# Windowed attention and mixed FFN on one core: projection weights in four column pieces, mixed-weight halves taken two steps behind, third pair's maxima sent ahead of the first loads of v

## The chip, the cores and the metric

The kernel runs on one NeuronCore of a Trainium2 chip, as one program. The core has a matrix engine (TensorE, PE in the profile; its weight loads are PEld), a vector engine (VectorE, DVE), a scalar engine (ScalarE, ACT), GpSimd (POOL) and SyncE (SP), which here only issues transfers. The metric is the device time of one execution in microseconds. Three runs of the kernel before took 3001.5, 3004.55 and 3013.76 us; the median is 3004.55 us.

## The reference, cut to what matters

```python
x = x + layernorm(attn(layernorm(x), w_qkv))       # x: 4 x 2048 x 512, w_qkv: 512 x 1536
x = x + layernorm(ffn(layernorm(x), ...))

# attn: 16 heads of 32 columns; queries in windows of 128 rows, each against the window
#       before, its own and the one after (384 keys; none beyond the ends of a sequence)
qkv = x @ w_qkv;  scores = (q * 32**-0.5) @ k_ctx.T;  out = softmax(scores) @ v_ctx

# ffn, per batch b of 4, with 8 experts
g   = mean over tokens of (relu(x @ gate_w1.T + gate_b1) @ gate_w2.T + gate_b2)   # 4 x 8
mW1 = W1 + sum_e g[b, e] * TW1[e];   mW2 = W2 + sum_e g[b, e] * TW2[e]            # F = 2048
u   = gelu(x @ mW1.T + b1 + g @ Tb1);   out = u @ mW2.T + b2 + g @ Tb2
```

Everything is float32. A layernorm is over the 512 columns.

## The kernel before, in words

Nearly every product is made three times to keep float32 accuracy: each operand is split into a high part (rounded to the matrix engine's `fp32r` by a copy on ACT) and a low part (the rest, a subtraction on DVE), and PE adds high by high, high by low and low by high. Every engine runs a fixed, written order of instructions; semaphores alone hold them together.

**Projection (to 581 us).** Sixteen chunks of 512 tokens. For each chunk DVE takes the row statistics and normalises (`take_stats`, `normalise_x`), PE transposes four blocks (`turn_block`, L529), ACT and DVE split them into `xt_hi` and `xt_lo` (`xt_block`, L346 and L441), and PE makes twelve groups of twelve products (`group`, L534): groups 0 to 3 are q, 4 to 7 are k (group g takes columns 128g to 128g+127 of the weights), groups 8 to 11 are v (columns 1024 to 1535). Groups 4 to 7 are followed by the transposes of the next chunk. Group 4 reuses the PSUM bank of group 0, and so waits until ACT and DVE have taken group 0 out.
Before the first chunk the weights are loaded by SP in four row blocks `k` of 128 rows and all 1536 columns (L233), right behind the first rows of x. ACT copies each block to `w_hi` (L378), DVE subtracts it for `w_lo` (L491). Both stand ahead of the first `xt_block` on their engines, and PE waits for all four before its first group (L665). The square root of the first statistics (L342) is the first activation of the program.

**Attention (581 to 1301 us).** Steps T, one pair of windows each. In step T PE makes the scores of pair T+3 (`score`, L585), the key products of pair T (`keys`, L602) and the output of pair T-2 (`values`, `sums`, L631, L639). DVE takes the maxima of the scores (`reduce`, L467); PE turns them (L610), DVE copies them to `max_rows` (L474) and SP sends them by two small transfers into one extra row of `q_st` (`row`, L228). `keys(g, 4)`, in the middle of a pair's eight, waits for the row of pair g+1. SP issues everything in its own order: at the change from projection to attention it sends the last stores of v (L201), then four loads of v of 256 KB (L215), then goes on with step 0, whose `row` is that of pair 2.

**Gate and FFN (1301 us to the end).** First sixteen chunks of normalising and gate. Then 256 steps s of about 5.4 us. A step is one block of 128 of the 2048 hidden columns, for one chunk of 512 tokens; two blocks are a run, so each odd step ends one. PE makes `hidden(s + 2)` (L1242 to L1244), then `project(s)` (L1259 to L1261). ACT makes gelu and high part of step s+2 (`hidden_block`, L1357, L1361); at the end of a run `next_run` copies four sums out (L1374) and puts the next four into PSUM (L1385), for which PE waits before the next `project`; three steps behind the last run of a chunk it normalises four tiles (`normalise`, L1399), after POOL has made the shift (L1132 to L1139) from DVE's statistics (L1586, L1589). DVE makes the low part `u_lo` of step s+2 (`low_hidden`, L1577) and, up to three times in a step, adds one expert to both halves of a weight block (`mix`, L1553, two instructions).
`mix_plan` gives, by fixed costs, the step `done[n]` in which weight block n has had its eight experts. `ready_by` says in which step the finished block is split: ACT makes `w_hi` (`high_weights`, L1350) and DVE `w_lo` (`low_weights`, L1572). A block that is wanted within two steps is split at the head of the step; else ACT does it behind `hidden_block` and `next_run` and ahead of `normalise`, and DVE behind the first addition of the step. A block is first used by `hidden` two steps ahead of its own step.

## Time and profile before

| | |
|---|---|
| runs | 3001.5, 3004.55, 3013.76 us; median 3004.55 |
| profiled execution | 3006.66 us; span of the instructions 3004.9 us |
| PE busy | 2890.8 us, 96% |
| DVE, ACT, POOL busy | 1988.1 (66%), 1727.3 (57%), 842.0 us (28%) |
| mean granted TensorE clock | 0.984 of 2.4 GHz |

PE is busy almost throughout, so the time is PE's work, the spans in which it waits, and the spans in which its granted clock is 0.50 (1.2 GHz) instead of 1.00 (2.4 GHz). What the other engines do costs only where PE waits for it. A busy PE's matmul ends are modelled, so the distance from start to start says more than the duration. "Idle before" in a row is the time the engine stood still ahead of it, with the engine and line that released it.

### The profile page before, as it was taken

To read this page: it belongs to the slowest core of one execution; us is meant where nothing else is said; L and a number is where in the kernel's file an instruction comes from. 1 tells how busy PE (TensorE), PEld (TensorE's weight loads), DVE (VectorE), ACT (ScalarE), POOL (GpSimd) and SP (SyncE) were. 2 spreads that over 40 slices of the span, in tenths; PEclk is the share of its full clock that TensorE was granted. 3 is DMA by queue.
4 is the path that set the end of the run, shared out by engine and by line. 5 is a ranking of instruction groups with operands and counts; after the bars stand their busy time and mean duration, and the time that the engine had idled before them with its cause. 6 is when DMAs were issued, how large, how long until landed. Compare 5 with 4: busy or idle time off the path is not lost.

```text
span 3004.9 us, 55697 instructions
## 1 busy us (share of the span) xinstructions
PE 2890.8 (96%) x20444; PEld 2414.2 (80%) x20444; DVE 1988.1 (66%) x3750; ACT 1727.3 (57%) x3384; POOL 842.0 (28%) x694
## 2 busy tenths in 40 slices
PE   7999999999999999959989999999999999999998
PEld 6888888788888888848777888888887888878886
DVE  4333333488877888858857767776669766786664
ACT  2222222376666667645645666766667666676665
POOL 1000000088888888853310000310005000040003
PEclk9999999999999999979999999999999999999999
DMA  5554555677887888769999766886669756896632
GB/s 194 184 180 169 176 187 199 203 181 188 195 187 188 195 196 193 172 206 389 381 359 345 258 231 228 330 318 234 218 216 392 255 201 215 287 358 214 238 133 84
DMA packets 363587, 697.06 MB, mean 232 GB/s; under 512 B 26424, under 2 KB 125752, under 8 KB 363336
## 3 DMA queue, kind: packets, MB, share of 16 engines
q1 hardware_dynamic: 342848, 646.15, 66.8%
q10 hardware_dynamic: 16416, 31.98, 3.0%
q0 software_dynamic: 4080, 15.73, 1.3%
q8 instruction: 148, 2.42, 0.3%
q14 instruction: 95, 0.78, 0.1%
HBM read 525.45 MB, written 167.78 MB: 231 GB/s over the span
## 4 chain that ended last, share of the span: by engine, by line
PE 45%; DMA 4%; ACT 2%; DVE 2%; issue 1%; POOL 1%; SPq 1%; POOLq 0%; ACTq 0%; DVEq 0%
PE e_hid L1242 7%; PE e_hid L1243 7%; PE e_hid L1244 7%; PE e_acc L1259 7%; PE e_acc L1260 7%; PE e_acc L1261 7%; DMA yl_scratch<-e_yt_lo 3%; POOL e_c_x L1127 1%; DVE e_part L1553 0%; SPq L1011 0%; ACT e_yt_hi L1321 0%; DVE e_c_stats L1476 0%; ACT e_sums L1374 0%; DMA e_att<-o_scratch 0%; ACT e_sums L1399 0%
## 5 line engine op out<-in xcount | busy, mean ns | idle before, releaser
L1553 DVE SCALAR_TENSOR_TENSOR e_part<-e_ring,e_g_cols,e_part 128x512 f32<-128x512 f32 x896 | 642.2, 776 | 3.8 <-DMA e_ring<-mix_rows 1.6
L467 DVE TENSOR_REDUCE a_neg_max<-a_ps_score 128x1 f32<-128x384 f32 (+1 forms) x1024 | 492.7, 527 | 67.4 <-PE a_ps_score L585 55.7
L312 POOL TENSOR_TENSOR a_total<-a_probs 128x512 f32<-128x512 f32 x256 | 323.7, 1281 | 620.2 <-ACT a_probs L397 620.2
L397 ACT ACTIVATE a_probs<-a_ps_keys 128x384 f32<-128x384 f32 (+1 forms) x1024 | 426.8, 478 | 56.5 <-PE a_ps_keys L602 29.5
L1357 ACT ACTIVATE e_u<-e_hid,e_mb 128x512 f32<-128x512 f32 x256 | 177.4, 693 | 446.3 <-PE e_hid L1244 440.2
L1577 DVE TENSOR_TENSOR e_u_lo<-e_u,e_u_hi 128x512 fp32r<-128x512 f32 x256 | 182.4, 712 | 317.3 <-ACT e_u_hi L1361 317.0
L1132 POOL TENSOR_SCALAR e_var<-e_moments 128x4 f32<-128x4 f32 x15 | 8.5, 566 | 1297.6 <-DVE e_moments L1589 1297.0
L602 PE MATMUL a_ps_keys<-a_q_st,a_k_st 97*128 97x384 f32 (+1 forms) x1024 | 314.2, 349 | 20.6 <-DMA a_q_st<-a_max_rows 18.9
L585 PE MATMUL a_ps_score<-a_k_st,a_q_st 96*128 96x384 f32 (+1 forms) x1024 | 326.6, 357 | 0.6 <-DVE a_neg_max L467 0.5
L322 POOL TENSOR_TENSOR a_total<-a_total,a_probs 128x512 f32<-128x512 f32 x224 | 286.2, 1278 | 68.8 <-ACT a_probs L397 66.3
L447 DVE TENSOR_TENSOR a_qk<-a_acc,a_qk 128x512 fp32r<-128x512 f32 x128 | 88.4, 690 | 315.8 <-ACT a_qk L353 315.8
L1374 ACT ACTIVATE e_sums<-e_acc 128x512 f32<-128x512 f32 x508 | 289.1, 595 | 5.7 <-PE e_acc L1261 5.7
L1385 ACT ACTIVATE e_acc<-e_sums 128x512 f32<-128x512 f32 x448 | 263.7, 614 | 0.0
L353 ACT ACTIVATE a_qk<-a_acc 128x512 fp32r<-128x512 f32 x128 | 76.6, 598 | 266.3 <-PE a_acc L534 266.3
L602 PEld LDWEIGHTS a_ps_keys<-a_q_st,a_k_st 97*128 97x128 f32 x1024 | 190.6, 191 | 34.5 <-DMA a_q_st<-a_max_rows 27.2
L585 PEld LDWEIGHTS a_ps_score<-a_k_st,a_q_st 96*128 96x128 f32 x1024 | 191.9, 190 | 27.7 <-DVE a_neg_max L467 16.9
L1259 PE MATMUL e_acc<-e_wa_hi,e_u_hi 128*128 128x512 f32 x512 | 201.5, 394 | 6.8 <-ACT e_acc L1385 6.8
L534 PE MATMUL a_acc<-a_xt_hi,a_w_hi 128*128 128x512 f32 x512 | 204.7, 400 | 1.4 <-DVE a_xt_lo L441 1.4
L1242 PE MATMUL e_hid<-e_y_hi,e_wb_hi 128*128 128x512 f32 x512 | 200.0, 391 | 2.3 <-DVE e_wb_lo L1572 2.3
L1242 PE MATMUL e_hid<-e_y_hi,e_wa_hi 128*128 128x512 f32 x512 | 200.7, 392 | 0.8 <-DVE e_x L1532 0.8
L1260 PE MATMUL e_acc<-e_wa_lo,e_u_hi 128*128 128x512 f32 x512 | 200.9, 392 | 0.0
L1261 PE MATMUL e_acc<-e_wa_hi,e_u_lo 128*128 128x512 f32 x512 | 200.6, 392 | 0.0
(147 smaller groups left out, 6510.4 us busy)
## 6 DMA issues: line engine op xcount, KB each, us to landing
e_ring<-mix_rows SPq DMA_DIRECT2D x558, 512.0 KB, 5.3
qk_scratch<-a_qk SPq DMA_DIRECT2D x128, 512.0 KB, 3.0
a_k_st<-qk_scratch SPq DMA_DIRECT2D x180, 256.0 KB, 4.3
a_q_st<-qk_scratch SPq DMA_DIRECT2D x180, 256.0 KB, 4.3
a_x_in<-x SPq DMA_DIRECT2D x16, 1024.0 KB, 7.1
v_scratch<-a_v SPq DMA_DIRECT2D x64, 256.0 KB, 3.1
a_v_sb<-v_scratch SPq DMA_DIRECT2D x64, 256.0 KB, 5.0
o_scratch<-a_out SPq DMA_DIRECT2D x128, 128.0 KB, 3.0
```

Of the source, the lines that this page charges most:

```text
L312: add = pool.tensor_tensor(total[:, g % 2, i], p[0], p[1], ALU.add)
L322: pool.tensor_tensor(total[:, g % 2, i], total[:, g % 2, i], p[2], ALU.add).then_inc(summed, 1)
L397: act.activation(probs[:, m % PROBS, h, 0:(hi - lo) * WIN], ps_keys[x % TRIO][:, 0:(hi - lo) * WIN], ACT.Exp, scale=SCALE).then_inc(exp_do ...
L467: dve.tensor_reduce(neg_max[:, g % 2, i, h:h + 1], ps_score[y % TRIO][:, 0:(hi - lo) * WIN], AX_X, ALU.max, negate=True).then_inc(reduced, 1)
L585: pe.matmul(ps_score[y % TRIO][:, 0:(hi - lo) * WIN], q_st[0:STACK, h, w * WIN:(w + 1) * WIN], k_st[0:STACK, h, lo * WIN:hi * WIN], start= ...
L602: pe.matmul(ps_keys[x % TRIO][:, 0:(hi - lo) * WIN], k_st[0:STACK + 1, h, w * WIN:(w + 1) * WIN], q_st[0:STACK + 1, h, lo * WIN:hi * WIN], ...
L1242: pe.matmul(hid[s % 4][:, :], w_hi(n)[:, 0, cols], y_hi[:, q, k, :], start=(k == 0), stop=False)
L1259: pe.matmul(acc[t][:, :], u_hi[:, s % 3, cols], w_hi(n)[:, 1, :], start=False, stop=False, skip_group_check=True)
L1260: pe.matmul(acc[t][:, :], u_hi[:, s % 3, cols], w_lo(n)[:, 1, :], start=False, stop=False, skip_group_check=True)
L1261: pe.matmul(acc[t][:, :], u_lo[:, s % 3, cols], w_hi(n)[:, 1, :], start=False, stop=end, skip_group_check=True).then_inc(used, 1)
L1374: act.activation(sums[:, runs[r][1], t, :], acc[t][:, :], ACT.Copy).then_inc(copied, 1)
L1553: dve.scalar_tensor_tensor(out=part[:, n % 2, half, :], in0=ring[:, slot, :], scalar=g_cols[:, b, e:e + 1], in1=so_far, op0=ALU.mult, op1= ...
```

## The change

- **Weights.** They come in pieces of columns 0 to 127, 128 to 511, 512 to 1023 and 1024 to 1535, all 512 rows each. SP issues the second piece after the first rows of x have landed. ACT and DVE split piece 0 ahead of the first `xt_block`s and the other three behind them. A small square root without a wait is put ahead of the first one on ACT. PE waits for a piece before groups 0, 1, 4 and 8 of the first chunk; for these waits the first two chunks are written out instead of being the first turn of the loop.
- **Maxima.** SP sends the row of pair 2 first, and then loads v.
- **FFN.** `ready_by` gives `done[n] + 2` instead of `done[n] + 1`.

```diff
+    PIECES = (0, P, D, 2 * D, 3 * D)
@@ SP
                 load_x(0, 0)
-                for k in range(KD):
-                    sp.dma_start(w_in[:, k, :], w_qkv[k * P:(k + 1) * P, :]).then_inc(w_loaded[k], 16)
+                for i in range(len(PIECES) - 1):
+                    cols = slice(PIECES[i], PIECES[i + 1])
+                    if i == 1:
+                        sp.wait_ge(x_loaded[0], 16)
+                    sp.dma_start(w_in[:, :, cols], w_qkv[:, cols].rearrange("(k p) n -> p k n", p=P)).then_inc(w_loaded[i], 16)
                 load_x(0, 1)
...
-                sp.wait_ge(v_done, TILES * (CHUNKS + 1))
-                for p in range(2):
-                    sp.wait_ge(v_stored[p], 16 * QUADS * 3)
-                for c in range(4):
-                    load_v(0, c)
                 for T in range(STEPS + LAG):
...
                     if there(T + AHEAD - 1):
                         row(T + AHEAD - 1)
+                    if T == 0:
+                        sp.wait_ge(v_done, TILES * (CHUNKS + 1))
+                        for p in range(2):
+                            sp.wait_ge(v_stored[p], 16 * QUADS * 3)
+                        for c in range(4):
+                            load_v(0, c)
@@ ACT
+                def split_weights(i):
+                    cols = slice(PIECES[i], PIECES[i + 1])
+                    act.wait_ge(w_loaded[i], 16)
+                    act.activation(w_hi[:, :, cols], w_in[:, :, cols], ACT.Copy).then_inc(w_hi_done, 1)
+
+                act.activation(unused[:, :], eps[:, :], ACT.Sqrt)
                 take_sqrt(1)
-                for k in range(KD):
-                    act.wait_ge(w_loaded[k], 16)
-                    act.activation(w_hi[:, k, :], w_in[:, k, :], ACT.Copy).then_inc(w_hi_done, 1)
+                split_weights(0)
                 for k in range(KD):
                     xt_block(0, 0, k)
+                for i in range(1, len(PIECES) - 1):
+                    split_weights(i)
@@ DVE
-                for k in range(KD):
-                    dve.wait_ge(w_hi_done, k + 1)
-                    dve.tensor_tensor(w_lo[:, k, :], w_in[:, k, :], w_hi[:, k, :], ALU.subtract).then_inc(w_lo_done, 1)
+                def split_weights(i):
+                    cols = slice(PIECES[i], PIECES[i + 1])
+                    dve.wait_ge(w_hi_done, i + 1)
+                    dve.tensor_tensor(w_lo[:, :, cols], w_in[:, :, cols], w_hi[:, :, cols], ALU.subtract).then_inc(w_lo_done, 1)
+
+                split_weights(0)
                 for k in range(KD):
                     xt_block(0, 0, k)
+                for i in range(1, len(PIECES) - 1):
+                    split_weights(i)
@@ PE
-                pe.wait_ge(w_lo_done, KD)
-                with pe.Fori(0, PAIRS - 1) as i:
+                for g in range(GROUPS):
+                    if g in (0, 1, QUADS, 2 * QUADS):
+                        pe.wait_ge(w_lo_done, (0, 1, QUADS, 2 * QUADS).index(g) + 1)
+                    group(0, 0, g)
+                    if QKG - KD <= g < QKG:
+                        turn_block(1, 1, g - (QKG - KD))
+                chunk(0, 1)
+                with pe.Fori(1, PAIRS - 1) as i:
@@ FFN
     def ready_by(s):
 
-        return [n for n in sorted(done) if max(done[n] + 1, 2) == s]
+        return [n for n in sorted(done) if max(done[n] + 2, 2) == s]
```

**DVE at the start of the program.** Before; `a_xn` are the normalised rows, `a_turn` the transposed blocks in PSUM:

```order
L35 BN_STATS a_stats<-a_x_in 128x6 x4
L40 BN_AGGR a_moments<-a_stats 128x2 x4
L430 RECIPROCAL a_rstd<-a_std 128x4
L435 TENSOR_SCALAR a_xn<-a_x_in,a_moments,a_rstd 128x512 x4
L491 TENSOR_TENSOR a_w_lo<-a_w_in,a_w_hi 128x1536 x4
L441 TENSOR_TENSOR a_xt_lo<-a_turn,a_xt_hi 128x512 x4
```

The same place now:

```order
L35 BN_STATS a_stats<-a_x_in 128x6 x4
L40 BN_AGGR a_moments<-a_stats 128x2 x4
L441 RECIPROCAL a_rstd<-a_std 128x4
L446 TENSOR_SCALAR a_xn<-a_x_in,a_moments,a_rstd 128x512 x4
L503 TENSOR_TENSOR a_w_lo<-a_w_in,a_w_hi 128x4x128
L452 TENSOR_TENSOR a_xt_lo<-a_turn,a_xt_hi 128x512 x4
L503 TENSOR_TENSOR a_w_lo<-a_w_in,a_w_hi 128x4x384
L503 TENSOR_TENSOR a_w_lo<-a_w_in,a_w_hi 128x4x512 x2
```

Of the 6144 columns of weights only 512 are still split ahead of the four `a_xt_lo`; ACT's order is changed in the same way.

**SP at the change from projection to attention.** Before; `a_max_rows` holds the maxima, two transfers for a pair of windows:

```order
L228 DMA a_q_st<-a_max_rows 1x4x128 x2
L201 DMA v_scratch<-a_v 128x4x128 x4
L215 DMA a_v_sb<-v_scratch 128x4x128 x4
L228 DMA a_q_st<-a_max_rows 1x4x128 x4
L172 DMA a_k_st<-qk_scratch 32x4x512 x3
```

The same place now:

```order
L229 DMA a_q_st<-a_max_rows 1x4x128 x2
L202 DMA v_scratch<-a_v 128x4x128 x4
L229 DMA a_q_st<-a_max_rows 1x4x128 x2
L216 DMA a_v_sb<-v_scratch 128x4x128 x4
L229 DMA a_q_st<-a_max_rows 1x4x128 x2
L173 DMA a_k_st<-qk_scratch 32x4x512 x3
```

The row of pair 2 stands ahead of the four loads of v, the row of pair 3 still behind them.

**ACT after the second batch, steps 130 and 131.** Before; `e_wb_hi` is the high part of weight block 35, `e_sums<-e_sums` is `normalise`, the rows from `e_sums<-e_acc` on are `next_run`:

```order
L1357 ACTIVATE e_u<-e_hid,e_mb 128x512
L1361 ACTIVATE e_u_hi<-e_u 128x512
L1350 ACTIVATE e_wb_hi<-e_part 128x1024
L1399 ACTIVATE e_sums<-e_sums,e_shift,e_rstd 128x512 x4
L1357 ACTIVATE e_u<-e_hid,e_mb 128x512
L1361 ACTIVATE e_u_hi<-e_u 128x512
L1374 ACTIVATE e_sums<-e_acc 128x512 x2
```

The same place now:

```order
L1379 ACTIVATE e_u<-e_hid,e_mb 128x512
L1383 ACTIVATE e_u_hi<-e_u 128x512
L1421 ACTIVATE e_sums<-e_sums,e_shift,e_rstd 128x512 x4
L1379 ACTIVATE e_u<-e_hid,e_mb 128x512
L1383 ACTIVATE e_u_hi<-e_u 128x512
L1396 ACTIVATE e_sums<-e_acc 128x512 x2
L1407 ACTIVATE e_acc<-e_bias 128x512
L1396 ACTIVATE e_sums<-e_acc 128x512
L1407 ACTIVATE e_acc<-e_bias 128x512
L1396 ACTIVATE e_sums<-e_acc 128x512
L1407 ACTIVATE e_acc<-e_bias 128x512 x2
L1372 ACTIVATE e_wb_hi<-e_part 128x1024
```

The split of block 35 now stands behind `normalise`, the next `hidden_block` and the whole `next_run`.

## Rows read from the trace of the kernel before

**Rows 1.** Waits of PE, whole span: us in total, times, longest.

```profile
PE a_ps_keys L602 <- DMA a_q_st<-a_max_rows: 18.9, 19, 4.8
PE e_acc L1259 <- ACT e_acc L1385: 7.1, 3, 3.5
```

**Rows 2.** Timeline, first 30 us: start, us, engine, line, operation [idle before].

```profile
9.45 1.28 ACT L342 ACT_TABLE_LOAD   x1 [9.45 <-DVE a_moments L40]
...
11.29 1.92 DVE L435 TENSOR_SCALAR a_xn<-a_x_in,a_moments,a_rstd 128x512 f32<-128x512 f32 x4
13.12 6.76 DVE L491 TENSOR_TENSOR a_w_lo<-a_w_in,a_w_hi 128x1536 fp32r<-128x1536 f32 x4
...
13.31 1.94 PE L529 MATMUL a_turn<-a_ident,a_xn 128*128 128x128 f32 x8 [13.31 <-DVE a_xn L435]
...
20.63 1.94 PE L529 MATMUL a_turn<-a_ident,a_xn 128*128 128x128 f32 x8 [5.38 <-DVE a_xt_lo L441]
...
22.38 0.69 DVE L441 TENSOR_TENSOR a_xt_lo<-a_turn,a_xt_hi 128x512 fp32r<-128x512 f32 x1 [1.30 <-ACT a_xt_hi L346]
...
23.98 0.80 PE L534 MATMUL a_acc<-a_xt_hi,a_w_hi 128*128 128x512 f32 x1 [1.41 <-DVE a_xt_lo L441]
...
28.34 0.40 PE L534 MATMUL a_acc<-a_xt_hi,a_w_hi 128*128 128x512 f32 x1
```

**Rows 3.** Timeline of SP, DVE and PE, 560 to 600 us.

```profile
584.41 3.04 SPq L215 DMA_DIRECT2D a_v_sb<-v_scratch  x4
587.49 2.43 SPq L228 DMA_DIRECT2D a_q_st<-a_max_rows  x4
...
583.81 0.27 DVE L474 CAST a_max_rows<-a_ps_turn 8x128 fp32r<-8x128 f32 x1
...
592.58 1.01 PE L602 MATMUL a_ps_keys<-a_q_st,a_k_st 97*128 97x384 f32 x2 [4.75 <-DMA a_q_st<-a_max_rows]
```

**Rows 4.** Transfers of the page: KB each, median us from issue to landing.

```profile
a_v_sb<-v_scratch SPq DMA_DIRECT2D x64, 256.0 KB, 5.0
o_scratch<-a_out SPq DMA_DIRECT2D x128, 128.0 KB, 3.0
```

**Rows 5.** Four stretches: us, busy us of each engine, PEclk, DMA share, GB/s.

```profile
592.50:600.50 8.00, 7.92 (x71) 6.91 (x72) 3.10 (x6) 3.29 (x8) 2.51 (x2) 0.50 0.42 100
1628.00:1631.00 3.00, 2.95 (x7) 2.37 (x8) 1.32 (x2) 0.00 (x0) 0.00 (x0) 0.52 1.02 408
2318.00:2321.00 3.00, 3.00 (x9) 2.28 (x7) 3.00 (x4) 2.20 (x4) 1.78 (x2) 0.50 1.05 416
2670.00:2675.50 5.50, 5.36 (x13) 4.23 (x14) 5.50 (x6) 3.76 (x7) 3.34 (x3) 0.50 1.04 410
```

**Rows 6.** Timeline of ACT, DVE, POOL and PE around 2310 us, PE at 2670.

```profile
2309.85 1.06 ACT L1350 ACTIVATE e_wb_hi<-e_part 128x1024 fp32r<-128x1024 f32 x1 [6.61 <-DVE e_part L1553]
2310.82 2.92 ACT L1399 ACTIVATE e_sums<-e_sums,e_shift,e_rstd 128x512 f32<-128x512 f32 x4
...
2303.87 0.61 POOL L1139 TENSOR_SCALAR e_shift<-e_shift 128x4 f32<-128x4 f32 x1
...
2316.11 1.76 DVE L1577 TENSOR_TENSOR e_u_lo<-e_u,e_u_hi 128x512 fp32r<-128x512 f32 x1
...
2316.58 0.47 PE L1259 MATMUL e_acc<-e_wa_hi,e_u_hi 128*128 128x512 f32 x1 [3.55 <-ACT e_acc L1385]
...
2670.14 0.77 PE L1259 MATMUL e_acc<-e_wa_hi,e_u_hi 128*128 128x512 f32 x1 [3.25 <-ACT e_acc L1385]
```

**Rows 7.** Timeline of DVE and PE, 1625 to 1629 us: weight block 3.

```profile
1625.44 1.42 DVE L1553 SCALAR_TENSOR_TENSOR e_part<-e_ring,e_g_cols 128x512 f32<-128x512 f32 x2
1626.77 1.23 DVE L1572 TENSOR_TENSOR e_wb_lo<-e_part,e_wb_hi 128x1024 fp32r<-128x1024 f32 x1
...
1628.05 0.78 PE L1242 MATMUL e_hid<-e_y_hi,e_wb_hi 128*128 128x512 f32 x1 [2.25 <-DVE e_wb_lo L1572]
```

**Rows 8.** Waits of DVE, 1550 to 3005 us.

```profile
DVE e_u_lo L1577 <- ACT e_u_hi L1361: 317.0, 123, 4.8
```

More of the change, by code:

```diff
@@ L110, in phase_qkv_attention @@
         ps_out = psum("ps_out", [P, 3, WIN])
-        w_loaded = [sem(f"w_loaded{k}") for k in range(KD)]
+        w_loaded = [sem(f"w_loaded{i}") for i in range(len(PIECES) - 1)]
         w_hi_done = sem("w_hi_done")
```

## The prediction, made before the changed kernel ran

> **What bounds the kernel now.** I read the page first: PE is busy 96% of the span. So the question of each edit is where PE stands still, and I went on to the waits of PE, where the reader is to see small sums in few places: 18.9 us for the rows of maxima, of which one wait alone is 4.8, and 7.1 us in three waits for ACT's preload of the sums, longest 3.5 [rows 1]. Then the timelines of these places. In each, the number to look for is the idle time before the PE row, and in the windows the column PEclk, since after such a stop PE runs at 0.50, that is at 1.2 instead of 2.4 GHz [rows 5].
>
> **Edit 1, the weights.** PE turns its first two blocks at 13.31 us and the next two only at 20.63, because DVE is busy 6.76 us with four low weight blocks before its first `xt_lo` [rows 2]. The first group of products starts at 23.98.
> - What goes: the pace of an undisturbed pair stands in the second pass. Transposes start at 20.63, DVE's next subtraction starts at 22.38 and takes 0.69, so it is done 2.44 us later. At this pace the second pass would follow the first after 2.44 us, and some 0.15 for the semaphore (an estimate: in the order the subtraction of one block comes just ahead of the transposes that it releases), together 2.6, instead of 20.63 - 13.31 = 7.32. That is 4.7 us.
> - The table load of 1.28 us stands between DVE's statistics and the first square root [rows 2]. It moves under the load of x: 1.3 us. A rule speaks for more: the Trainium skill, "ScalarE: Activation LUTs", What ACT_TABLE_LOAD costs, puts a switch at some 2.66 us, as the load is followed by a drain of nearly its own length; by it this term would be 2.7. The row shows the load alone, with the activation of the square root right behind it, so the row decides.
> - What is added: a quarter-size piece on each engine ahead of the first `xt` block. On DVE a piece 0 of 512 columns takes a twelfth of 6.76, 0.6 to 0.7 us; it starts when xn is done, and so does PE's transposing, whose first block ACT and DVE cannot take out for over a microsecond. Nothing.
> - What is late next: with 6.0 us gained, group 0 starts at 18.0 and lasts 28.34 - 23.98 = 4.4, until 22.3. Piece 1 (a quarter of the columns) must be split by then: DVE ends `xt_lo` at about 17.9, ACT has begun 0.7 earlier and needs a quarter of four 1.5 us copies (estimated from DVE's 1.7 for the same size), DVE 1.7 behind it: about 20.4. It fits by 2 us. Pieces 2 and 3 take DVE until 25, and groups 4 and 8 come at about 30 and 41. Behind them on DVE stand the statistics of chunk 1 (2.9 us) and then group 0's low part, at about 29.4, while group 4 wants its bank at 30.5. This slack of about 1 us is the thinnest; if the clock rose earlier than before, PE would meet it.
> - x may land up to 0.7 us earlier, since only piece 0 is queued with it; on the other side the delayed pieces could come late.
> I take 6.0, between 4.0 and 8.0. The first bound is the 4.7 less a stop of 0.7 at group 1 or 4, the second adds the earlier x and part of the slow clock before 27 us.
>
> **Edit 2, the maxima.** DVE has copied the row of pair 2 at 584.1 (583.81 + 0.27), but SP issues four loads of v from 584.41 and the row at 587.49. PE stands from 587.82 to 592.58, so the row came 5.09 us after its issue [rows 3], as long as the v loads just ahead of it (5.0) and much longer than the 3.0 of a store out of SBUF [rows 4]. Now it is issued at about 584.4. With 5.1 us it lands at 589.5 and PE waits 1.7; with 3.0 at 587.4 and PE does not wait. I take 0.6: the wait falls by 4.2.
> - Afterwards PE ran 8.0 us at 0.50 [rows 5]. Half of that is 4.0 us; but at full clock DVE's maxima would hold it part of the time, so I take 3.0, between 0 (the clock falls all the same) and 4.0.
> - Queued behind the row: the v loads start 1.2 us later (two issues of 0.6, 2.43 us for four). They are wanted by `values(0)`, at about 591 in the new time, and the first lands at 585.6 + 5.0 = 590.6. Just in time.
> - What is late next: the row of pair 3, still issued behind the loads of v at about 588.7, as before. It lands at about 593.8, and `keys(2, 4)` gets there at about 593.3. I charge 0.5.
> Sum: 4.2 + 3.0 - 0.5 = 6.7, between 2 and 8.
>
> **Edit 3, the split of the mixed weights.** PE waits in three places of the FFN on this chain.
> - After batches 2 and 3: ACT, in step 130, waits 6.61 us for DVE's last addition to block 35, then splits it (2309.85), then normalises (2.92 us), then does step 133's gelu and only then `next_run`, for which PE stands 3.55 us. At 2670 the same with 3.25 us [rows 6]. Behind them PE runs 3.0 and 5.5 us at 0.50 [rows 5], which costs 1.5 and 2.75, and 0.2 for the edges. Together 3.55 + 3.25 + 1.5 + 2.75 + 0.2 = 11.3 us. Now the split stands behind `next_run` (ACT in the order rows), and nothing else that ACT does there needs block 35: the shift for `normalise` is ready on POOL at 2304.5 [rows 6], so ACT is done with it before 2308 and free for `next_run`, wanted from about 2310 on. What is late next there: DVE. It ends its `u_lo` at 2317.9 (2316.11 + 1.76) [rows 6], and without the stop PE wants that one at about 2318.3. But DVE also gets ahead: the wait for ACT's part of block 34 and its own split of 35 (1.2 us) leave the stretch. I take the whole 11.3, with 0 as the other bound if DVE is the next to hold it.
> - Block 3, at the start of the FFN: DVE has no slack there. Its addition, split and addition run back to back, and PE already stands 2.25 us for the split [rows 7]. `low_weights(3)` now stands behind one more addition of both halves: 1626.77 - 1625.44 = 1.33 us, less about 0.2 of a wait for block 2's split that goes. PE waits 1.1 longer. The stretch at 0.52 behind it [rows 5] may grow to that of the longer stops, 0 to 1.3. I charge 1.6, between 1.1 and 2.4.
> - The other 59 blocks: PE waits for none, before; a block is split one step of 5.4 us later and is used five steps later still. On most of them ACT's split moves out of the odd steps, where it stood behind `next_run`, to the even ones. No gain, no loss.
> Sum: 11.3 - 1.6 = 9.7, between -2.4 and 11.
>
> **The sum.** 6.0 + 6.7 + 9.7 = 22.4 us. The profiled execution took 3006.66 us, so 2984.3 by it. It lay 2.1 above the median of the runs, so the median would be 2982. I say 2983.
>
> **The rivals.**
> - *DVE holds the batch ends (A).* The stop for ACT is replaced by one for `u_lo`: DVE's row ends at 2317.9, only 0.4 before it is wanted, and while POOL adds, DVE's instructions are slow (1.76 us for a subtraction that takes 0.69 [rows 2]). Against it: DVE loses two pieces of work ahead of it. Edit 3 would then leave -1.6: 3006.7 - 12.7 + 1.6 = 2995.6 by the profile, 2993 by the median.
> - *The row of pair 3 takes the wait of pair 2 (B).* It is behind the four loads of v, which themselves start later. If it lands 5.1 us behind the last of its issues at 589.9, that is 595, PE stops 1.7 and may fall back to 0.50 for half as long as before. Edit 2 gives 6.7 - 1.2 - 2.0 = 3.5, and 1.5 with the clock down all of the time: gains of 19.2 to 17.2, medians of 2985 to 2987. The Trainium skill speaks for this one: "DMA: Bandwidth & Descriptors", Queues, rings and completion order, has all of SP's transfers on one row of rings, whose descriptors are taken in order, so a small one starts behind the large ones. By that rule, the trace agrees so far: the row of pair 2 landed with the loads ahead of it.
> - *The start does not move (C).* If PE's first group still begins near 24, because the first xn or x waits on something else, the median is 2982 + 6 = 2988. The rows leave little room.
> - *Slower (D).* The later splits hold DVE's `low_hidden` for PE. DVE does 62 splits of 1.2 us. It stood idle 317 us for ACT's `u_hi` in 123 of the 256 steps [rows 8], so it has room on average; but if the moved split came between `u_hi` and `u_lo` wherever that room is missing and each stood on PE's path, it would cost 62 x 1.2 = 74 us: 3004.6 - 12.7 + 74 = 3066. It decides from 12.7 / 62 = 0.2 us a block. Against it, PE waits for no `u_lo` at all before, and `low_hidden` stands ahead of the split in each step.
>
> **How the numbers follow.** Forecast 0.66, A 0.16, B 0.10, C 0.03, D 0.05. The range of 2975 to 2999 holds the forecast's own spread (edits 1 and 2 at their bounds with edit 3 at 9.7 give gains of 15.7 to 25.7, medians of 2979 to 2989), B, C and A, and leaves out D and the far ends. A measurement of this kernel can tell about 0.5%, 15 us, from no change: the line is 2989.5. Faster: 0.66 of the forecast, 0.08 of B and 0.02 of C, 0.76. Slower: D, 0.05. The same: A and what is left of B and C, 0.19.
>
> **What would show it.** The first `a_acc` group at about 18 us, and no PE wait at the three later pieces. At the change of phase a PE wait below 1.7 us instead of 4.75 and PEclk near 1.00 behind it; the next suspect is a wait for `a_max_rows` in the step after. No PE wait for the preload of the sums (L1385 before) behind batches 2 and 3; at block 3 a wait of about 3.4 instead of 2.25. It would be wrong if PE waits for `e_u_lo` at the batch ends, or if waits for `e_wa_lo` or `e_wb_lo` show up behind block 3.

## The result and the profile after

The changed kernel took 2993.67 us (median of 13 runs, 2983.01 to 3010.66); the kernel before, run beside it, 3007.61 (13 runs). The ratio is 0.9949, 95% interval 0.9934 to 0.9964: 15.3 us less (the ratio's distance from 1 times the median of before; by the interval 10.8 to 19.8), where 22.4 were forecast. Its profiled span is 2995.2 us, 9.7 under the 3004.9 of before.

The trace, cut at the first product of the projection, its last, the last instruction of PE in the attention and the first `hidden` of the FFN's steps behind the wait for `e_x` (1584.66 us before, 1579.14 after), in us:

| | first product | projection | attention | gate | FFN |
|---|---|---|---|---|---|
| before | 23.98 | 557.3 | 719.8 | 283.6 | 1420.2 |
| after | 17.76 | 557.2 | 715.1 | 289.2 | 1416.1 |

So 6.2 us come from the start, 4.7 from the attention and 4.1 from the FFN, and the gate, whose code is the same, took 5.6 more in this execution. The waits of PE in the changed kernel (us in total, times, longest), beside [rows 1]:

```profile
PE a_ps_keys L618 <- DMA a_q_st<-a_max_rows: 14.7, 20, 1.9
...
PE e_hid L1264 <- DVE e_wb_lo L1594: 3.2, 1, 3.2
PE e_acc L1281 <- DVE e_u_lo L1599: 2.6, 1, 2.6
PE e_hid L1264 <- DVE e_wa_lo L1594: 2.2, 1, 2.2
```

The wait of 4.8 for a row of maxima and the two for the preload of `e_acc` behind batches 2 and 3 (3.55 and 3.25) are gone. Two that before did not have, for `e_u_lo` and for `e_wa_lo`, have come.

**The start.** Timeline of ACT, DVE and PE, beside [rows 2]:

```profile
0.81 1.28 ACT L385 ACT_TABLE_LOAD   x1 [0.81 <-PEq L1758]
...
9.17 0.30 ACT L347 ACTIVATE a_std<-a_moments,a_eps 128x4 f32<-128x4 f32 x1 [6.86 <-DVE a_moments L40]
...
11.54 0.68 DVE L503 TENSOR_TENSOR a_w_lo<-a_w_in,a_w_hi 128x512 fp32r<-128x512 f32 x1
...
14.31 1.94 PE L545 MATMUL a_turn<-a_ident,a_xn 128*128 128x128 f32 x8 [0.65 <-DVE a_xt_lo L452]
17.76 0.76 PE L550 MATMUL a_acc<-a_xt_hi,a_w_hi 128*128 128x512 f32 x1 [1.50 <-DVE a_xt_lo L452]
```

The second pass of transposes waits 0.65 us instead of 5.38, the first product comes at 17.76 instead of 23.98, and PE never stops for a piece of weights.

**The change of phase.** SP's issues and PE, beside [rows 3], and then the windows behind the stop (us, busy us of PE, PEld, DVE, ACT, POOL, PEclk, DMA share, GB/s):

```profile
577.99 1.65 SPq L229 DMA_DIRECT2D a_q_st<-a_max_rows  x2
579.77 2.05 SPq L216 DMA_DIRECT2D a_v_sb<-v_scratch  x4
581.86 1.20 SPq L229 DMA_DIRECT2D a_q_st<-a_max_rows  x2
...
588.84 0.61 PE L618 MATMUL a_ps_keys<-a_q_st,a_k_st 97*128 97x384 f32 x2 [1.91 <-DMA a_q_st<-a_max_rows]
```

```profile
591.00:594.50 3.50, 3.50 (x49) 2.93 (x52) 2.30 (x6) 1.49 (x4) 2.51 (x2) 0.54 0.38 106
...
1623.06:1626.00 2.94, 2.94 (x13) 2.40 (x14) 0.00 (x0) 0.00 (x0) 0.00 (x0) 1.00 1.01 389
1669.16:1672.00 2.84, 2.84 (x7) 2.25 (x8) 1.28 (x2) 0.00 (x0) 0.00 (x0) 0.55 1.02 365
1964.87:1968.00 3.13, 3.13 (x10) 2.52 (x11) 3.13 (x6) 1.77 (x3) 0.00 (x0) 0.74 1.02 294
```

Pair 2's row no longer holds PE. Pair 3's, issued behind the four loads, does for 1.91 us, and the clock falls to 0.54 for 3.5 us. From the last product of the projection to the fourth turning of maxima on PE (`a_ps_turn<-a_ident,a_neg_max`) it is 24.6 us before and 20.3 now: 4.3 us less at this place.

**The FFN.** Stops of PE at block 3, at block 5 and behind batch 1; with them DVE at block 5, and DVE and POOL behind batch 1:

```profile
1623.06 0.50 PE L1264 MATMUL e_hid<-e_y_hi,e_wb_hi 128*128 128x512 f32 x1 [3.24 <-DVE e_wb_lo L1594]
...
1669.16 0.60 PE L1264 MATMUL e_hid<-e_y_hi,e_wa_hi 128*128 128x512 f32 x1 [2.25 <-DVE e_wa_lo L1594]
...
1964.87 0.50 PE L1281 MATMUL e_acc<-e_wa_hi,e_u_hi 128*128 128x512 f32 x1 [2.61 <-DVE e_u_lo L1599]
```

```profile
1666.57 1.41 DVE L1575 SCALAR_TENSOR_TENSOR e_part<-e_ring,e_g_cols,e_part 128x512 f32<-128x512 f32 x2
1667.90 1.21 DVE L1594 TENSOR_TENSOR e_wa_lo<-e_part,e_wa_hi 128x1024 fp32r<-128x1024 f32 x1
...
1951.48 1.21 DVE L1594 TENSOR_TENSOR e_wb_lo<-e_part,e_wb_hi 128x1024 fp32r<-128x1024 f32 x1
...
1953.21 11.00 DVE L1575 SCALAR_TENSOR_TENSOR e_part<-e_ring,e_g_cols,e_part 128x512 f32<-128x512 f32 x6
1964.14 0.68 DVE L1599 TENSOR_TENSOR e_u_lo<-e_u,e_u_hi 128x512 fp32r<-128x512 f32 x1
...
1953.35 3.46 POOL L1171 TENSOR_TENSOR e_sums<-e_sums,e_x 128x512 f32<-128x512 f32 x2
...
1957.97 5.02 POOL L1171 TENSOR_TENSOR e_sums<-e_sums,e_x 128x512 f32<-128x512 f32 x4
```

At block 5 one more pair of additions stands ahead of the split, as at block 3. Behind batch 1 DVE's three additions (six instructions, a mix from here on) take 11.00 us while POOL makes six of its own, and `u_lo` is late behind them. The 11.00 us are not six equal parts. Asked for the middle of them alone (window 1958.5 to 1962.5), the timeline shows one single instruction:

```profile
1957.94 5.61 DVE L1575 SCALAR_TENSOR_TENSOR e_part<-e_ring,e_g_cols,e_part 128x512 f32<-128x512 f32 x1
```

It spans POOL's last four additions (1957.97 to 1962.99). All six stops of PE for `e_u_lo` over 1 us in this study (here, in e3_twobehind, and two each in e5_two_blocks and e8_best) stand behind such an instruction, of 5.6 to 6.3 us. It alone makes no stop: e2_maxima has one of 5.62 us and PE does not wait behind it.

A finer ruler for the FFN: the distance between ACT's gelu rows eight steps apart is 43.52 us where nothing stops PE, and 43.25 across the end of a batch. At the batch ends and at the start of the FFN, in us:

| gelu of steps | before | two behind alone | after | 35, 51 | 34, 35, 50, 51 |
|---|---|---|---|---|---|
| 64 to 72 (batch 1) | 43.26 | 48.55 | 47.94 | 43.25 | 43.25 |
| 128 to 136 (batch 2) | 48.25 | 42.93 | 43.23 | 47.78 | 43.25 |
| 192 to 200 (batch 3) | 49.13 | 42.88 | 42.50 | 45.25 | 43.25 |
| 8 to 32 (blocks 3, 5) | 134.71 | 138.30 | 138.29 | 133.11 | 134.99 |

"Two behind alone", "35, 51" and the last column are e3_twobehind, e5_two_blocks and e9_four_blocks, told below. Before to after: batches 2 and 3 give 5.02 + 6.63 = 11.65 us, batch 1 takes 4.68 and blocks 3 and 5 take 3.58. The last figure hides part of its price: behind the same stop of 2.25 us at block 3 the clock was 0.52 before [rows 5], but 1.00 in e4_edits12 (1609.73 to 1612.73 us), whose stretch is 133.15.

### The profile page after: what moved, and what is told of

It is laid out like the page before. It is cut to its first block, busy times and chain, and to the rows that moved or that the text cites. A ratio compares the mean times of both kernels' runs of the same rounds, so it can differ in the third digit from the quotient of the medians.

```text
span 2995.2 us, 55675 instructions
## 1 busy us (share of the span) xinstructions
PE 2892.5 (97%) x20444; PEld 2414.3 (81%) x20444; DVE 1989.4 (66%) x3750; ACT 1730.8 (58%) x3385; POOL 838.4 (28%) x694
## 4 chain that ended last, share of the span: by engine, by line
PE 46%; DVE 3%; DMA 3%; SPq 1%; ACT 1%; issue 1%; POOL 1%; POOLq 0%; ACTq 0%; DVEq 0%
PE e_hid L1264 8%; PE e_hid L1265 7%; PE e_hid L1266 7%; PE e_acc L1281 7%; PE e_acc L1282 7%; PE e_acc L1283 7%; DMA yl_scratch<-e_yt_lo 2%; POOL e_c_x L1149 1%; DVE e_c_stats L1498 1%; DVE e_part L1575 1%; SPq L1033 1%; DVE e_c_y L1519 0%; DMA e_att<-o_scratch 0%; ACT e_yt_hi L1343 0%; PE e_hid L1245 0%
## 5 line engine op out<-in xcount | busy, mean ns | idle before, releaser
L327 POOL TENSOR_TENSOR a_total<-a_total,a_probs 128x512 f32<-128x512 f32 x224 | 286.2, 1278 | 68.9 <-ACT a_probs L408 66.3
L1396 ACT ACTIVATE e_sums<-e_acc 128x512 f32<-128x512 f32 x508 | 289.2, 595 | 7.5 <-PE e_acc L1283 7.5
L1265 PE MATMUL e_hid<-e_y_lo,e_wa_hi 128*128 128x512 f32 x512 | 201.7, 394 | 0.0
L1266 PE MATMUL e_hid<-e_y_hi,e_wa_lo 128*128 128x512 f32 x512 | 201.1, 393 | 0.0
```

The lines of the kernel that those rows point to most:

```text
L327: pool.tensor_tensor(total[:, g % 2, i], total[:, g % 2, i], p[2], ALU.add).then_inc(summed, 1)
L1265: pe.matmul(hid[s % 4][:, :], w_hi(n)[:, 0, cols], y_lo[:, q, k, :], start=False, stop=False)
L1266: mm = pe.matmul(hid[s % 4][:, :], w_lo(n)[:, 0, cols], y_hi[:, q, k, :], start=False, stop=(k == KD - 1))
L1396: act.activation(sums[:, runs[r][1], t, :], acc[t][:, :], ACT.Copy).then_inc(copied, 1)
```

## The experiments

Times are medians; the gain in us is the ratio's distance from 1 times the median of before beside it (3006.17, 3003.88 and 3004.07 us for the three groups), its interval in brackets.

| run | time | ratio | gain |
|---|---|---|---|
| e1_weights | 2994.73 | 0.9966 | 10.2 [6.6, 13.5] |
| e2_maxima | 3001.32 | 0.9990 | 3.0 [-0.6, 6.6] |
| e3_twobehind | 3003.37 | 0.9993 | 2.1 [-2.1, 6.0] |
| e4_edits12 | 2988.57 | 0.9949 | 15.3 [10.5, 20.1] |
| e5_two_blocks | 2985.94 | 0.9933 | 20.1 [16.2, 23.7] |
| e6_row3 | 2985.60 | 0.9937 | 18.9 [15.0, 22.5] |
| e7_rows_first | 2994.16 | 0.9962 | 11.4 [6.9, 15.6] |
| e8_best | 2990.81 | 0.9952 | 14.4 [9.9, 18.6] |
| e9_four_blocks | 2975.65 | 0.9900 | 30.0 [24.3, 35.7] |
| e12_peel_only | 3000.88 | 0.9984 | 4.8 [1.2, 8.4] |

### Each edit alone

Edit 1 alone (before, with all its lines):

> The kernel before with the weights edit alone. Theory 1 (the start moves by itself and everything behind it follows): first group of products at 17.8 us instead of 24.0, last score of the projection's end 6.3 us earlier, the wait of PE for the row of pair 2 still 4.8 us; time 6 us less, ratio 0.998. Rival (the start's gain is taken back where transfers set the pace, in the gate): the same 6.3 us at the end of the projection, but the stretch from the last attention product to the first hidden product grows from 283.6 us to 289 us as it did in the changed kernel, and the time is the same as before, ratio 1.000.

The first product came at 17.78 and the projection ended 5.9 us earlier (575.34 for 581.26). The rival fell: the gate took 286.1 us, and it was no part of the edit, since with the other two edits alone it took 287.5 and 286.2. Over all 14 traces of this study the gate lies between 282.2 and 289.2 us, before's 283.6 and after's 289.2 near the ends: 5.6 us of scatter that the two profiles had set down as a loss. But the run gave 10.2 us, more than the start's 6.2. The rest lies in the attention, 712.4 us for 719.8, and comes up again below.

Edit 2 alone:

> The kernel before with the maxima edit alone (row of pair 2 ahead of the four loads of v). Prediction: wait for pair 2 goes from 4.8 to under 1 us, pair 3 about 0.5, clock stays up: 6.7 us less at the end of attention. Rival B: the row of pair 3, still behind the loads of v, takes a wait of about 1.9 us and the clock falls behind it: 4 to 5 us less at the end of attention. In both the stretch of the gate stays near 283.6 us unless it varies from one execution to the next.

Pair 2's wait was gone, pair 3's was 1.04 us, and the clock stayed at 1.00 behind it. To the fourth turning of maxima it is 17.9 us here for 24.6 before, 6.7 less, as forecast. But the whole attention took 717.7 us, only 2.1 less: later waits for rows have grown, 16.3 us behind 600 us for 14.2. The traced execution was the slowest of its twelve (3008.99 us). The prediction's 6.7 is just outside the interval of the time, rival B's 3.5 inside; zero is inside too.

Edit 3 alone:

> The kernel before with mixed-weight halves split two steps behind, alone. Prediction: the FFN (first hidden product to the end) 9.7 us shorter than 1420.2. Theory from the changed kernel's trace: only 4 us shorter, because new stops of PE of 3.2 us at block 3, of 2.2 us at block 5 (for e_wa_lo) and of 2.6 us behind batch 1 (for e_u_lo) take most of the 7 us that the stops behind batches 2 and 3 cost. Rival: those new stops are chance of one execution; then block 5 and batch 1 show no stop here and the FFN is 9 to 10 us shorter. Time 4 or 10 us less.

Its waits of PE in the FFN:

```profile
PE e_acc L1259 <- DVE e_u_lo L1577: 3.3, 1, 3.3
PE e_hid L1242 <- DVE e_wb_lo L1572: 3.2, 1, 3.2
PE e_hid L1242 <- DVE e_wa_lo L1572: 2.3, 1, 2.3
```

The same three stops as in the changed kernel at the same steps (that for `u_lo` 3.3 us instead of 2.6): they belong to the edit, not to chance. FFN 1416.7 us, 3.5 less than before; in time 2.1 us, which the measurement can't tell from nothing.

Edits 1 and 2 together:

```diff
-        return [n for n in sorted(done) if max(done[n] + 2, 2) == s]
+        return [n for n in sorted(done) if max(done[n] + 1, 2) == s]
```

> The changed kernel with the split one step behind, as before (edits 1 and 2 without 3). If the gains add: start 6.3 and attention 4.7 us, 11 us less than before, and the FFN has its stops of 3.5 and 3.3 us behind batches 2 and 3 again and none behind batch 1 or at block 5. If the changed kernel's edit 3 is worth its 4 us the time is 10 to 11 us less than before (ratio 0.9964); if the gate takes back what comes earlier, 5 us (0.9983).

The same ratio as the changed kernel: edit 3 added nothing that can be measured. The FFN took 1416.8 us with the old stops, as in the other traces of the one-step form behind edit 1 (1416.3 to 1417.4), and the changed kernel 1416.1. So most of the 4.1 us that the first two profiles show for the FFN is not edit 3's: 1.6 of it is the clock behind block 3 (gelu 8 to 32 took 134.71 us before and 133.15 here, with the same stop). The one-step form without edit 1 has 1420.2 (before) and 1419.8 (e2_maxima), with the written-out pair alone (e12_peel_only, below) 1416.1; what makes this difference isn't settled.

### The split of the mixed weights

```diff
-        return [n for n in sorted(done) if max(done[n] + 2, 2) == s]
+        return [n for n in sorted(done) if max(done[n] + (2 if n in (35, 51) else 1), 2) == s]
```

> The changed kernel with two steps behind for weight blocks 35 and 51 alone, whose split stood ahead of the normalising after batches 2 and 3; all others one step behind. Theory (the prediction's mechanism was right there, and the other sixty blocks gave it back at block 3, block 5 and behind batch 1): no PE stop over 1 us in the FFN but the 2.25 us at block 3, FFN from the mean of the looks of the one-step form (1418.4 us) to 1408 to 1411, 6 to 8 us under the changed kernel's 1416.1; the time 20 us under before, ratio 0.993. Rival (any stop taken away in the FFN comes back within a few steps, since DVE is the real bound there): stops appear behind batch 1, 2 or 3 for e_u_lo and the FFN stays at 1416.

Batch 1 and block 5 were free again, as expected, but the rival held at the ends of batches 2 and 3, and the FFN took 1412.6 us, between the theory's 1408 to 1411 and the rival's 1416:

```profile
PE e_acc L1281 <- DVE e_u_lo L1599: 4.6, 2, 2.6
PE e_hid L1264 <- DVE e_wb_lo L1594: 2.3, 1, 2.3
```

Both groups of POOL's additions fell on DVE's six-instruction mix (DVE and POOL, batch 2):

```profile
2283.33 1.23 DVE L1594 TENSOR_TENSOR e_wb_lo<-e_part,e_wb_hi 128x1024 fp32r<-128x1024 f32 x1 [2.84 <-ACT e_wb_hi L1372]
...
2294.37 11.66 DVE L1575 SCALAR_TENSOR_TENSOR e_part<-e_ring,e_g_cols,e_part 128x512 f32<-128x512 f32 x6
...
2295.17 3.46 POOL L1171 TENSOR_TENSOR e_sums<-e_sums,e_x 128x512 f32<-128x512 f32 x2
...
2299.79 5.01 POOL L1171 TENSOR_TENSOR e_sums<-e_sums,e_x 128x512 f32<-128x512 f32 x4
```

The same place in the changed kernel, where block 34 is late as well:

```profile
2303.12 6.14 DVE L1575 SCALAR_TENSOR_TENSOR e_part<-e_ring,e_g_cols,e_part 128x512 f32<-128x512 f32 x6
...
2303.27 3.46 POOL L1171 TENSOR_TENSOR e_sums<-e_sums,e_x 128x512 f32<-128x512 f32 x2
...
2310.36 6.44 POOL L1171 TENSOR_TENSOR e_sums<-e_sums,e_x 128x512 f32<-128x512 f32 x4 [2.49 <-DMA e_x<-x_scratch]
```

The difference is when DVE comes to the mix, seen from ACT's gelu behind it (2298.66 and 2309.96 us): 4.3 us ahead of it in e5_two_blocks, 6.8 in the changed kernel. In e5_two_blocks DVE had stood 2.84 us for ACT's high part of block 34, the first row above; in the changed kernel that split comes later and DVE waits for nothing there. So its mix, and POOL's first two additions, are over early; POOL then waits 2.49 us for the rows of x, and its last four additions miss the mix: 6.14 us instead of 11.66. (The load of these rows was issued earlier, not later: 13.0 us ahead of the gelu, for 9.0 in e5_two_blocks.)

Behind batch 1 the moved split works the other way. It stands right ahead of the mix (1951.48 above), which starts 3.6 us ahead of ACT's next gelu (1956.86) instead of 7.0 before (1952.08 for 1959.11), and POOL's last four additions, which before just missed it (1958.38, with the mix over at 1958.22), fall on it. Before, DVE and POOL there:

```profile
1952.08 6.14 DVE L1553 SCALAR_TENSOR_TENSOR e_part<-e_ring,e_g_cols,e_part 128x512 f32<-128x512 f32 x6
...
1958.38 6.71 POOL L1149 TENSOR_TENSOR e_sums<-e_sums,e_x 128x512 f32<-128x512 f32 x4 [0.90 <-DMA e_x<-x_scratch]
```

All this is read from the rows. Whether POOL's additions are what makes `u_lo` late was tried by making them small, in the changed kernel, which leaves out the residual of the other 448 columns there:

```diff
-                    rows = sums[:, runs[closing[at]][1], t, :]
-                    pool.tensor_tensor(rows, rows, x1[:, at % 2, t, :], ALU.add).then_inc(added, 1)
+                    rows = sums[:, runs[closing[at]][1], t, 0:64]
+                    pool.tensor_tensor(rows, rows, x1[:, at % 2, t, 0:64], ALU.add).then_inc(added, 1)
```

> The changed kernel, but POOL adds x to 64 of the 512 columns of each tile at the batch ends (the residual of the other columns is left out). Theory (POOL's six additions on DVE's six-instruction mix are what makes it 11.0 us instead of 4.05): the mix behind batch 1 takes 4 to 5 us, the PE stop of 2.61 us for e_u_lo is gone, and the FFN is 4 us shorter, 1412 us. Rival (the late split's order alone makes u_lo late): the mix may be shorter, but the stop stays over 1.5 us.

The stop behind batch 1 was gone, and the mix there was not slow (DVE, then POOL):

```profile
1935.60 4.20 DVE L1575 SCALAR_TENSOR_TENSOR e_part<-e_ring,e_g_cols,e_part 128x512 f32<-128x512 f32 x6
1940.43 0.69 DVE L1599 TENSOR_TENSOR e_u_lo<-e_u,e_u_hi 128x512 fp32r<-128x512 f32 x1 [0.63 <-ACT e_u_hi L1383]
...
1936.41 1.51 POOL L1171 TENSOR_TENSOR e_sums<-e_sums,e_x 128x64 f32<-128x64 f32 x2
...
1944.44 1.16 POOL L1171 TENSOR_TENSOR e_sums<-e_sums,e_x 128x64 f32<-128x64 f32 x4 [5.38 <-DMA e_x<-x_scratch]
```

The mix took 4.20 us for 11.00, and `u_lo` now waits for ACT. The FFN was 1410.6 us (1412 expected) although the stop at block 3 was 4.4 us this time. It is one execution, 2977.65 us. POOL's last four additions also came later here, outside the mix, so this run does not part their size from their place. What it does show: with the same late split and without POOL's long additions on the mix there is no stop. The order of the split by itself does not make `u_lo` late.

Then the four blocks, on top of e6_row3 (next part):

```diff
-        return [n for n in sorted(done) if max(done[n] + 1, 2) == s]
+        return [n for n in sorted(done) if max(done[n] + (2 if n in (34, 35, 50, 51) else 1), 2) == s]
```

> Edits 1 and 2, the row of pair 3 ahead of the later loads of v, and two steps behind for weight blocks 34, 35, 50 and 51 alone. In the changed kernel the ends of batches 2 and 3, where these four were late, had no stop, and with 35 and 51 alone they had stops of 2.6 and 2.0 us for e_u_lo. Theory: the additions of POOL fall on DVE's three-addition step unless ACT's normalising is held or split by the load of e_x; with the four blocks late both ends are free, batch 1 and block 5 stay free, and only the 2.25 us at block 3 is left: FFN 1408 to 1410 us, time 2978 to 2982, ratio 0.992. Rival: the free ends of the changed kernel hung on its other late blocks too; then u_lo stops come back, FFN 1412 us, time 2985.

All that PE waits for in the FFN over 0.1 us:

```profile
PE e_hid L1266 <- DVE e_wb_lo L1596: 2.7, 1, 2.7
PE e_acc L1283 <- ACT e_acc L1409: 0.3, 1, 0.3
```

FFN 1408.1 us, as the theory had it, each batch end at the free pace, although the clock was 0.50 for 3 us behind the stop at block 3. The time is below the theory's 2978 to 2982 us. The median of 2975.65 us is the lowest of the study, and its ratio (0.9900, to 0.9919) lies clear of the changed kernel's (0.9949, from 0.9934). It is the version to keep.

### The rows of maxima

```diff
                     if T == 0:
...
-                        for c in range(4):
-                            load_v(0, c)
+                        load_v(0, 0)
+                    if T == 1:
+                        for c in range(1, 4):
+                            load_v(0, c)
```

> Edits 1 and 2 with the split one step behind, and the row of pair 3 sent ahead of the loads of v but the first. If pair 3's row waited behind the loads (rival B's mechanism), the PE wait of 1.6 to 1.9 us for it falls under 0.6 and the clock stays at 1.00 behind it: 1.5 to 4 us less than edits 1 and 2 alone in the attention. If it only comes as late as DVE makes it, the wait stays.

SP's issues, and the window behind:

```profile
580.85 0.40 SPq L216 DMA_DIRECT2D a_v_sb<-v_scratch  x1
582.78 1.19 SPq L229 DMA_DIRECT2D a_q_st<-a_max_rows  x2
584.01 1.54 SPq L216 DMA_DIRECT2D a_v_sb<-v_scratch  x3
```

```profile
586.00:600.00 14.00, 14.00 (x229) 12.22 (x222) 11.10 (x29) 9.58 (x23) 13.16 (x12) 1.00 0.81 204
```

Between 560 and 620 us PE waits for no row any more, and the clock stays at 1.00. The row is not issued earlier than in the changed kernel (6.76 us behind the projection's last product for 6.95), only with one load ahead of it instead of four. e9_four_blocks has this order and no wait there either; in the five traces with the four loads ahead (e2_maxima, e5_two_blocks, e4_edits12, the changed kernel, e10_narrow_adds) PE waits 1.02 to 2.39 us for this row. So rival B's mechanism is shown. Its clock is not: only the changed kernel's fell, and behind the 2.39 us of e10_narrow_adds it stayed at 1.00. In time the 3.6 us over e4_edits12 lie within the two intervals.

If loads ahead of a row cost 1.91 us there, they might cost the other 10 us of such waits too. In every step SP now sends `row(T + AHEAD - 1)` first and then that step's `load_k`, `load_q` and `load_v`:

> As the last one, and in every step SP sends the row of maxima ahead of that step's loads of k, q and v. Theory (the 10 to 19 us that PE waits for rows in the attention are SP's issue of loads, 3.1 us in odd steps, and the loads themselves, standing ahead of the row): the sum of these waits falls from 10.2 (edits 1 and 2) to under 4 us, no slow clock in the attention, which takes 697 us instead of 705.6 to 720; the time 5 to 9 us under edits 1 and 2. Rival (the rows land late because loads of the step before share the rings): sum stays near 10 us, time the same. Loads that come later may make PE wait for v or k; then those waits show.

Waits of PE in the attention, first of e4_edits12, then of this kernel:

```profile
PE a_ps_keys L618 <- DMA a_q_st<-a_max_rows: 10.2, 15, 1.6
```

```profile
PE a_ps_score L603 <- DMA a_q_st<-qk_scratch: 10.0, 15, 1.4
PE a_ps_score L603 <- issue: 2.8, 5, 0.9
```

No wait for a row is left. The loads of q took its place, again with 10 us in 15 waits, and 2.8 more: here the order on SP decides only who waits. It is 7.5 us slower than e6_row3 (the intervals overlap by 0.6 us). The theory lost: the waits for rows did go, but its gain went to the late loads, and the time is worse than the rival's too.

> The two last ideas together: rows first in every step, and two steps behind for blocks 35 and 51 alone. If both theories hold: attention 697 us and FFN 1409 us, time about 2977 us, ratio 0.990; if only the FFN part holds 2983; if only the rows 2981.

2990.81 us: the stops of e5_two_blocks (2.9 and 2.0 us for `e_u_lo`) and the waits of e7_rows_first, 713.5 us of attention, in one kernel. None of its three forecasts held.

### The start and the written-out pair

Edit 1 without the early square root:

> Edit 1 alone without the square root put ahead. By the row (table load of 1.28 us, moved under the load of x) the first group of products starts at 17.78 + 1.3 = 19.1 us. By the page of the Trainium skill (ScalarE: Activation LUTs, 2.66 us for a switch with its drain) it would be 20.4.

```profile
9.10 1.28 ACT L346 ACT_TABLE_LOAD   x1 [9.10 <-DVE a_moments L40]
...
18.99 0.76 PE L548 MATMUL a_acc<-a_xt_hi,a_w_hi 128*128 128x512 f32 x1 [1.50 <-DVE a_xt_lo L450]
```

18.99 us against 17.78: 1.21 us, the row's 1.28. The square root starts at 10.40 here, right behind the load. The 2.66 us that the Trainium skill gives for a switch ("ScalarE: Activation LUTs", What ACT_TABLE_LOAD costs) do not show at this place (one execution of this kernel, 2994.43 us).

Before, with nothing changed but PE's first pair of chunks written out:

```diff
                 pe.wait_ge(w_lo_done, KD)
-                with pe.Fori(0, PAIRS - 1) as i:
+                for g in range(GROUPS):
+                    group(0, 0, g)
+                    if QKG - KD <= g < QKG:
+                        turn_block(1, 1, g - (QKG - KD))
+                chunk(0, 1)
+                with pe.Fori(1, PAIRS - 1) as i:
```

> The kernel before with nothing changed but PE's first two chunks written out instead of looped; the weights as before. In the five looks with edit 1 the attention took 705.6 to 715.1 us, in the three without it 717.7 to 719.9. Rival 1 (PE's code is what shortens it): attention under 716 us here and the time 4 to 8 us under before. Rival 2 (the start that comes earlier, or the pieces' transfers, or chance): attention 717 to 720 us, the time as before, ratio 1.000.

4.8 us [1.2, 8.4] less, and an attention of 713.1 us: rival 1. All eleven traces with the written-out pair have an attention of 705.6 to 715.1 us, the three without it 717.7 to 719.9. The same PE work in the same order, in other places of its program, makes the waits for rows between 600 and 1305 us smaller (this kernel, then e3_twobehind, whose attention code is that of before):

```profile
PE a_ps_keys L602 <- DMA a_q_st<-a_max_rows: 9.8, 18, 0.9
```

```profile
PE a_ps_keys L602 <- DMA a_q_st<-a_max_rows: 14.4, 18, 2.6
```

In the three traces without the written-out pair they are 14.2, 14.4 and 16.3 us; in the nine with it in which rows are waited for, 8.5 to 13.1. How the writing-out does it isn't settled.

## Why the prediction was right in kind and too high in size

- **Edit 1: 6.0 forecast, 10.2 measured [6.6, 13.5].** Its steps held one by one: the second pass of transposes came 2.6 us behind the first as forecast, the first group at 17.76 for 18.0, no stop at a piece, the table load worth 1.2. What was missing is a term: writing out PE's first pair is not in the sum at all and gave 4.8 [1.2, 8.4]. The rest, 5.4, is close to the 6.0.
- **Edit 2: 6.7 forecast, 3.0 measured [-0.6, 6.6].** The wait for pair 2 fell by all of 4.75 us. The charge of 0.5 for the row of pair 3 was mis-sized: 1.91 in the changed kernel, 1.64 in e4_edits12, 1.04 in e2_maxima, in the first with a clock of 0.54 for 3.5 us behind it, 1.6 us more (3.5 x 0.46). At the change of phase the edit then gives 4.3 us in the changed kernel and 6.7 in e2_maxima. So there the forecast was reached once; the median says 3.0 all the same, and what takes the rest back, later in the attention, isn't shown. The wait for pair 3 was rival B, given a tenth. By the rule of the Trainium skill named there ("DMA: Bandwidth & Descriptors", Queues, rings and completion order), e6_row3 agrees: ahead of three of the loads, the row is in time.
- **Edit 3: 9.7 forecast, 2.1 measured [-2.1, 6.0].** The 11.3 us of the batch ends came as forecast, 11.65 by the gelu rows (11.94 against e4_edits12). The step that failed is "The other 59 blocks: no gain, no loss". Block 5 stands where block 3 does, one extra pair of additions ahead of the split with no slack: 2.24 us. Batch 1 cost 4.68: there the moved split stood right ahead of DVE's mix and made it late, so that POOL's six additions all fell on it. That is rival A's mechanism, at a batch end where before had no stop and where the prediction looks for none. Block 3 itself waited 3.24 for 3.4, and the clock behind it stayed at 1.00 (0.75 in e3_twobehind, 1631.79 to 1634.79 us). Rival D's 74 us never threatened: five places decide, not 62.
- **The sum.** 10.2 + 3.0 + 2.1 = 15.3 for the three alone, and 15.3 together. With intervals of 3.3 to 4.8 us to either side this shows no interplay, but can't exclude one: edits 1 and 2 together also gave 15.3, where 13.2 would be the sum. The forecast was 7.1 higher: edit 3 7.6 and edit 2 3.7 too high, edit 1 4.2 too low.
- **Luck in the number.** Without the 4.8 us of the written-out pair, which nobody forecast, the gain would have been about 10.5 us, less than half of the 22.4. The median of 2993.67 us is rival A's 2993 (given 0.16), above the forecast's own spread of 2979 to 2989. Rival A had the right kind of stop, for `u_lo`, but behind batches 2 and 3, where the changed kernel has none; its number came by another sum. The 15 us that the prediction takes for what a measurement can tell were too many: the interval here is 4.5 us to either side.

## What to carry to other kernels

When work is moved by a rule over all blocks, walk all places where it lands and not only the one that it is meant for: here the four blocks at two batch ends were worth 11 us and the other moved ones cost 8. Before a queue is put in another order, ask who waits for what is now last; in the attention the wait changed its name and not its length (10.2 us for rows, then 10.0 for q). Look at the single instructions inside a merged row: the mean of the six was 1.83 us, and one of them took 5.61. And time each edit alone: the first two profiles differed by 5.6 us in a stage that nobody had touched.

## What the runs showed of the hardware

- DVE's additions of two 128x512 tensors take 0.74 us each by themselves (0.68 from start to start) and 1.78 where each alternates with one of POOL's (POOL's then 1.74). But one DVE addition can also stand while four of POOL's pass: 5.61 us in the changed kernel (1957.94), 6.26 in e5_two_blocks (2299.10), and POOL's took 1.26 to 1.31 each meanwhile, the 1.29 that they take with DVE idle (2275.48 in the changed kernel). What decides between the two patterns isn't settled. The Trainium skill ("SBUF — State Buffer", SBUF: two separate sides) gives a shared pair of ports to whichever instruction starts first, for the whole of it, and lets the other engine wait, where DVE's has two inputs in SBUF and POOL's reads SBUF; these rows agree: the addition of 5.61 us ends at 1963.55, 0.56 us behind the last of POOL's four.
- The granted clock behind a stop of PE is no function of the stop's length. In the changed kernel it was 1.00 after 3.24 us, 0.55 after 2.25, 0.74 after 2.61, and after 1.91 it fell 2 us later. The stop of 2.25 us at block 3 is the same in ten traces of the one-step form: in seven the clock stayed at 1.00 for the 3 us behind it, in three it was 0.50 to 0.54 (before, e2_maxima, e6_row3), with 1.6 us more to the next gelu. It was at 0.50 at once behind each stop of over 4 us (4.34 to 5.12, at the change of phase and at block 3 of e10_narrow_adds).
- A change of PE's program that leaves its work as it was moved the time by 4.8 us [1.2, 8.4]. The medians of two of the three edits alone are smaller.
